# An LSTM recurrence whose turned gate sums move from SBUF to PSUM

## The reference

```python
xW = jnp.einsum('ntd,dg->ntg', x, Wx) + b
def step(carry, xw_t):
    prev_h, prev_c = carry
    a = xw_t + prev_h @ Wh
    i = sigmoid(a[:, :H]); f = sigmoid(a[:, H:2*H]); o = sigmoid(a[:, 2*H:3*H])
    g = tanh(a[:, 3*H:])
    next_c = f * prev_c + i * g
    next_h = o * tanh(next_c)
    return (next_h, next_c), next_h
x = x + lstm(x, h0=cond)
ys = cond / 16
d = rsqrt(einsum('bi,io->bo', ys*ys, weight*weight) + 1e-8)
out = x + einsum('bsi,io->bso', x * ys[:, None, :], weight) * d[:, None, :]
```

## Time and profile before

| | |
|---|---|
| median of 3 runs | 2243.52 us (2242.71 to 2243.88) |
| the profiled execution's own time | 2243.01 us |
| its span in the trace | 2241.2 us |
| PE, DVE, ACT, POOL busy | 69%, 63%, 38%, 5% of the span |
| first to last transpose | 26.7 to 2221.2 us |
| granted TensorE clock | full, 1.0 |

### The profile page before, as it was taken

How to read it: one execution, slowest core, us unless ns; L and a number is a source line. 1 busy time by engine, 2 the same in 40 slices (tenths; PEclk the granted TensorE clock), 3 DMA queues, 4 the chain that set the end, 5 groups by cost and what they waited for, 6 DMA issues and landing times.

```text
span 2241.2 us, 121713 instructions
## 1 busy us (share of the span) xinstructions
PE 1542.8 (69%) x49800; PEld 1253.7 (56%) x49800; DVE 1404.2 (63%) x12314; ACT 855.0 (38%) x4100; POOL 116.3 (5%) x648
## 2 busy tenths in 40 slices
PE   5666666666666666666666666666666666666666
PEld 4555555555555555555555555555555555555554
DVE  4666666666666666666666666666666666666665
ACT  2333333333333333333333333333333333333332
POOL 0000000000000000000000000000000000000000
PEclk9999999999999999999999999999999999999999
DMA  2000000000000000000000000000000000000000
GB/s 82 0 0 0 0 0 0 0 0 0 0 0 0 0 0 0 0 0 0 0 0 0 0 0 0 0 0 0 0 0 0 0 0 0 0 0 0 0 0 37
DMA packets 4428, 6.70 MB, mean 3 GB/s; under 512 B 1089, under 2 KB 2881, under 8 KB 4418
## 3 DMA queue, kind: packets, MB, share of 16 engines
q1 hardware_dynamic: 3872, 5.51, 0.7%
q10 hardware_dynamic: 546, 1.05, 0.1%
HBM read 4.46 MB, written 2.10 MB: 3 GB/s over the span
## 4 chain that ended last, share of the span: by engine, by line
DVE 46%; PE 37%; ACT 10%; issue 6%; DMA 0%; SPq 0%; POOLq 0%; POOL 0%
PE pA L179 36%; DVE turned L276 29%; DVE junk L281 11%; ACT gates L151 10%; DVE hst L289 5%; DVE gates L281 1%; PE pO L231 1%; DMA w_sb<-in_w_dram 0%; PE pD L160 0%; SPq L99 0%; PE pD L187 0%; PE pA L170 0%; PE pA L167 0%; DVE ores L297 0%; DVE wsq L256 0%
## 5 line engine op out<-in xcount | busy, mean ns | idle before, releaser
L179 PE MATMUL pA<-wh_sb,hst 128*2 128x128 f32 (+3 forms) x40960 | 1092.7, 252 | 676.7 <-DVE hst L289 676.7
L179 PEld LDWEIGHTS pA<-wh_sb,hst 128*2 128x2 f32 (+1 forms) x40960 | 793.5, 90 | 956.0 <-DVE hst L289 951.3
L276 DVE STREAM_TRANSPOSE turned<-pA 128x128 f32<-128x128 f32 x2048 | 650.2, 317 | 561.0 <-PE pA L179 548.5
L151 ACT ACTIVATE gates<-turned 128x8 f32<-128x8 f32 x2048 | 442.3, 216 | 1222.1 <-DVE turned L276 1106.1
L281 DVE CUSTOM_DVE_ANT_0 junk<-gates 128x4 f32<-128x4 f32 x4096 | 504.6, 161 | 76.5
L155 ACT ACTIVATE tanhc<-gates 128x2 f32<-128x2 f32 x2048 | 418.2, 204 | 128.2
L160 PE MATMUL pD<-wh_sb,ones 128*32 128x128 f32 x2608 | 452.5, 273 | 0.0
L289 DVE TENSOR_TENSOR hst<-tanhc,gates 128x2 f32<-128x2 f32 x2048 | 330.9, 162 | 172.1 <-ACT tanhc L155 172.1
L281 DVE DVE_READ_ACCUMULATOR2_ANT gates<- 128x1 f32 x4096 | 340.3, 83 | 0.0
L160 PEld LDWEIGHTS pD<-wh_sb,ones 128*32 128x32 f32 x2608 | 285.8, 110 | 1.0
L170 PE MATMUL pA<-wx_sb,xr 128*16 128x128 f32 x4128 | 207.9, 274 | 0.0
(11 more groups left out here) (24 smaller groups left out, 9.6 us busy)
## 6 DMA issues: line engine op xcount, KB each, us to landing
outT_dram<-ores SPq DMA_DIRECT2D x8, 256.0 KB, 2.5
xh<-in_xT_dram SPq DMA_DIRECT2D x6, 320.0 KB, 7.9
wx_sb<-in_Wx_dram SPq DMA_DIRECT2D x1, 1024.0 KB, 5.2
wh_sb<-in_Wh_dram ACTq DMA_DIRECT2D x1, 1024.0 KB, 7.6
w_sb<-in_w_dram SPq DMA_DIRECT2D x1, 256.0 KB, 8.4
xh<-in_xT_dram SPq DMA_DIRECT2D x2, 64.0 KB, 7.5
condT<-in_condT_dram ACTq DMA_DIRECT2D x1, 2.0 KB, 5.4
bias_sb<-in_bT_dram ACTq DMA_DIRECT2D x1, 4.0 KB
```

The lines of the kernel that those rows point to most:

```text
L151: act.activation(gates[:, j, :, 0:3 * G:3].rearrange("p b g -> p g b"), turned[:, j, :, B * t:B * (t + 1)], ACT.Sigmoid).then_inc(gates_re ...
L179: last = pe.matmul(pA[st][j][c * Q:c * Q + M, lo * Q:hi * Q].rearrange("p (g u) -> p g u", u=Q), hst[:, st, k, Q * t:Q * t + M], chunk(wh_ ...
L276: dve.transpose(turned[:, j, :, :].rearrange("p g r -> p (g r)"), pA[st][j][:, 0:P]).then_inc(turned_ready[j], 1)
```

## The change

Two more PSUM tensors `pT[0]` and `pT[1]`, a bank each, replace the SBUF tensor `turned`. Transpose `j` writes the first 128 columns of `pT[j]`, and sigmoid `j` reads its 8 columns there. To have eight banks suffice, `pD` is no longer a bank of its own but another name for `pO[1]`, which is otherwise used only in the linear layer behind the loop. The sigmoids' output, the cell state, the constants in `gates`, `tanhc` and `hst` stay in SBUF. No instruction is added or removed, and each engine issues them in the same order with the same waits.

```diff
-        turned = sb("turned", [P, K, G, Q])
...
-        pD = ctx.enter_context(nc.psum_tensor("pD", [P, 512], F32))
+        pT = [ctx.enter_context(nc.psum_tensor(f"pT{j}", [P, 512], F32)) for j in range(K)]
         pO = [ctx.enter_context(nc.psum_tensor(f"pO{n}", [P, 512], F32)) for n in range(2)]
+
+        pD = pO[1]
+        turned = [pT[j][:, 0:G * Q].rearrange("p (g r) -> p g r", g=G) for j in range(K)]
...
                         act.activation(gates[:, j, :, 0:3 * G:3].rearrange("p b g -> p g b"),
-                                       turned[:, j, :, B * t:B * (t + 1)], ACT.Sigmoid).then_inc(gates_ready[j], 1)
+                                       turned[j][:, :, B * t:B * (t + 1)], ACT.Sigmoid).then_inc(gates_ready[j], 1)
...
-                        dve.transpose(turned[:, j, :, :].rearrange("p g r -> p (g r)"),
+                        dve.transpose(pT[j][:, 0:G * Q],
                                       pA[st][j][:, 0:P]).then_inc(turned_ready[j], 1)
```

## The result

The changed kernel takes 2226.99 us (median of 6 runs, 2226.10 to 2228.85) where the kernel before takes 2243.13 us (6 runs): a ratio of 0.9928, 95% interval 0.9916 to 0.9941, or 16 us less. The profiled execution took 2228.85 us, its span is 2227.1 us.

A forecast was written before the change was run, and what follows sets the result against it. The prediction took one turn of the ring, 1024 times, to bound the kernel, both halves critical. Sigmoids' saving of 20 ns and transposes' loss of 0 gave -20.5 us, 2223 against the 2243.52 median; range 2204 to 2284, its own 2213 to 2239.

The forecast's parts named there:

- What bounds the kernel: Whole kernel: no engine over 69% busy, TensorE clock full; each engine waits 1024 times for the one before it.
- One turn of the ring: One loop step through TensorE, transpose, sigmoid, cell, tanh and state, back to the next step's transpose: 2.145 us.
- (1): Sigmoids read PSUM instead of SBUF: 20 ns saved a turn, assumed about midway between 7 and 43.
- (2): Transposes write PSUM instead of SBUF: loss taken as 0 ns, at most 59, or -7 by the small pair.
- (3): The sum: the paths through both halves change alike, -20 ns x 1024 = -20.5 us, forecast 2223.
- path B: The chain through half 1, transpose 1 to state 1 and TensorE's second-half products; critical too, with some 10 ns of slack.
- What holds transpose 1: Start of transpose 1: it waits for its sums, 0.34 us behind record 40; transpose 0's end just before is coincidence.
- VectorE's overlap as the bound for cell 0: Cell 0 behind transpose 1: VectorE's next instruction starts some 0.085 us before the last ends, so only 0.035 earlier.
- R1: Sigmoids' read saves near 43 ns, transposes' write costs 0; cell 0 starts 35 ns sooner: 36 us, 2207; chance 15 in 100.
- R2: Transposes' slower PSUM write outweighs the sigmoids' saving: loss of 5 to 40 us, up to 2284; chance 22 in 100.
- R3: No sigmoid saving with full write loss, 2304 us, or transposes not overlapping, 2334; chance 13 in 100 together.
- R4: Operand's memory hardly matters: sigmoids' saving within 4 ns of transposes' loss, 2239 to 2248 us; chance 17 in 100.

The follow-up runs named there:

- half 0 alone: Against the changed kernel, only half 0 goes through PSUM, half 1 through SBUF as before; 2243.7 us, ratio 0.9995.
- the sigmoids' read alone: Against the changed kernel, transposes write SBUF and sigmoids read an idle PSUM bank of zeros; 2210.6 us, ratio 0.9847.

## Why the prediction came out right

- **What bounds the kernel**: right. One turn of the ring times 1024 is the time, and no engine's busy time is.
- **(1), the sigmoids' read**: right in sign. I took 20 ns between the bounds of 7 and 43; it is 32 to 33. The row from which 7 came (VectorE out of PSUM) was no guide for ScalarE, the 43 of ScalarE's longer fixed time was the nearer. By its own signs of being right, sigmoids of about 196 ns, this term failed: they are at 183 or 184.
- **(2), the transposes' write**: I took 0 between -7 and 59; the transposes took 13 to 14 ns more and the turn 15, where the sign of being right was that they stay at 316 to 319 ns. I had let a read out of PSUM stand for a write into it. The two terms missed by about 13 ns each, in opposite directions, so that the sum, -20 ns, was closer than its parts deserved: that the forecast of 2223 is only 4 us from 2227 is luck.
- **(3), both paths alike**: right, with one false step inside. I gave path B a slack of some 10 ns, from starts rounded to 10 ns. The run of half 0 alone shows that what can be had from it is 1 ns. In the loop's mean record 17 begins 60 ns behind state 1's end in the kernel before and 55 with half 0 alone, so the slack is 5 ns, and the records behind the hold take 4 of them back. It did no harm, as the change moves both paths.
- **What holds transpose 1**: its own sums, as the 0.34 behind record 40 says before and after. Freed of them and given another bank it starts 0.09 earlier, and the turn doesn't change; that run doesn't part the wait from the bank.
- **VectorE's overlap as the bound for cell 0**: shown at 0.08 in the run with the sigmoids' read alone. In that run cell 0 starts 0.24 behind transpose 1. In the changed kernel it starts 0.25 behind it, and 32 ns behind sigmoid 0's end as before, so the bound doesn't limit it, but it is near.
- **R1** was nearer in the saving, 32 to 33 of its 43 ns, and failed by the write. **R2** had the right direction, a dearer write, at less than a quarter of its bound: it would decide from 33 ns on. Why the write is dearer no run shows.
- **R3** fell on both counts: the saving is there and transposes overlap. **R4** fell, since the read gains ScalarE 33 ns and the write costs VectorE 13.
- Perfetto Trace Analysis, a page of the Trainium skill, in its section on optimizing Scalar and DVE operations, gives access costs from which the prediction had two estimates, 42 ns less for ScalarE and 65 more for VectorE. Both signs were right for what this change does. Here the runs show 32 to 33 and 13 to 14, so that the sum has the other sign.

## What to carry to other kernels

In a ring of small instructions, price the memory of each operand by the engine that touches it, and a read apart from a write: here ScalarE gained 32 ns for reading PSUM and 28 for writing it, and VectorE lost 13 for writing a 128x128 transpose there and nothing for reading 2 to 4 elements. Look at who reads and who writes before moving a tensor: a value from ScalarE to VectorE, the tanh here, gave 32 ns a turn, and one from VectorE to ScalarE, the turned sums, gave 17. Where two halves go round the same ring, shorten one alone first as an experiment: when neither alone gives anything, both are critical, and only a change to both pays.

## What the runs showed of the hardware

**Matmuls held between two groups ran 4 ns longer behind the hold.** With half 0 alone through PSUM, records 1 to 40 took 1.09 us instead of 1.06 to 1.07, and the turn gained 1 ns of the 19 by which TensorE started earlier. The longer wait for the second half is 12 of them. Another 4 lie behind it: records 17 to 40 take 464 ns in the loop's mean and 459 to 460 in all ten other traces. That the hold is the cause of these 4 is argued from this one version, not tried apart.

**Both ends of the kernel scatter by a few us, whatever the loop does.** In the changed kernel's profiled run the first transpose came at 27.9 us, where it was 26.7 before, and TensorE's granted clock was at 1.0 in the loop but at its lower level (1.2 GHz) for part of the tail. Busy us of PE, PEld, DVE, ACT and POOL with counts, then the granted clock, the DMA share and GB/s:

```profile
2206.60:2209.00 2.40, 1.31 (x2) 0.64 (x3) 0.00 (x0) 0.00 (x0) 0.70 (x4) 0.82 0.00 0
2209.00:2214.00 5.00, 5.00 (x10) 2.15 (x9) 1.50 (x2) 0.00 (x0) 0.00 (x0) 0.75 0.14 52
2214.00:2219.00 5.00, 5.00 (x13) 2.19 (x12) 2.25 (x3) 0.00 (x0) 0.00 (x0) 1.00 0.41 157
```

At full clock 13 records fit in 5 us, at 0.75 only 10. TensorE had waited for the last residual additions before the clock fell, as it had in the kernel before, where it stayed at full in the same place. The two profiled spans differ by 14.1 us: the loop's 17.1 less 1.2 at the start and 1.8 at the end.

The other runs point the same way. In the five profiled runs whose mean granted clock is 0.999, VectorE waits 11.5 us for the linear layer; in the six with 1.0, 9.8 or 9.9 us. The runs of the unchanged kernel beside the experiments fall into two groups, 2242.3 to 2243.5 us at 1.0 and 2244.1 to 2245.9 at 0.999. All three medians of before lie in the upper group, and those of most edited kernels among runs at 1.0. That fits the loop's 17 us showing as 18.9, and 32 as 34.4, in differences of medians. So 1 to 3 us of any difference here can't be told from medians or from two profiles; the turn can, to about 1 ns.
